# A self product computed as a fifth seven-block relation, and matrix sums moved to accumulating transfers

## The reference, cut to what matters

```python
# layer 0: three hops over a row-normalised adjacency
cur = h = x @ W + b;  out = dw[0] * h
for i in range(3):
    cur = adj @ cur;  out = out + dw[i+1] * cur
x = x + relu(out);  h = relu(layernorm(x))
# layer 1: four relations, 16384 weighted edges
for r in range(4):
    total_msg += (h[src] @ W_rel[r] + b_rel[r]) * where(edge_type == r, edge_weight, 0)[:, None]
agg = segment_sum(total_msg, dst) / maximum(segment_sum(edge_weight, dst), 1)[:, None]
h1 = h @ W_self + b_self + agg            # then layernorm, a feed-forward block, layernorm
```

## Time and profile before

| what | value |
|---|---|
| time before, median of 3 runs | 346.32 us (345.88 to 346.45) |
| the profiled execution's own time | 345.88 us |
| its span | 343.6 us |
| TensorE busy | 336.5 us (98% of the span) |
| VectorE busy | 243.2 us (71%) |
| GpSimd busy | 153.0 us (45%) |
| ScalarE busy | 87.1 us (25%) |
| chain that ended last, by engine | TensorE 88%, VectorE 8%, ScalarE 1% |
| granted TensorE clock | 0.9 or more of full speed in every slice |

### The profile page before, as it was taken

The page is one execution under the profiler, slowest core; times in us unless marked ns, Lnnn a source line. Parts: engine busy times, 40 slices in busy tenths (PEclk is TensorE's granted clock), DMA queues, the critical chain, the costliest instruction groups (busy, mean ns, idle before and its releaser), DMA issues.

```text
span 343.6 us, 4413 instructions
## 1 busy us (share of the span) xinstructions
PE 336.5 (98%) x1624; PEld 239.5 (70%) x1625; DVE 243.2 (71%) x428; ACT 87.1 (25%) x187; POOL 153.0 (45%) x122
## 2 busy tenths in 40 slices
PE   7999999999999999999999999999999999999996
PEld 3459887785478888888888888844774544474455
DVE  5899999988596898691484598786676555443543
ACT  3565664333410000000001062223352331112110
POOL 6000000461379999999936220491115440772020
PEclk9999999999999999999999999999999999999999
DMA  7100002728800000062300089942000000000003
GB/s 240 66 1 2 5 2 85 284 57 216 279 0 2 0 1 0 2 245 65 59 0 2 0 283 190 139 141 73 1 2 0 1 0 0 2 0 0 2 0 124
DMA packets 18630, 22.07 MB, mean 64 GB/s; under 512 B 2032, under 2 KB 10992, under 8 KB 18608
## 3 DMA queue, kind: packets, MB, share of 16 engines
q1 hardware_dynamic: 17936, 20.72, 21.6%
q0 software_dynamic: 240, 0.79, 0.8%
q10 hardware_dynamic: 432, 0.26, 0.2%
HBM read 20.72 MB, written 1.05 MB: 63 GB/s over the span
## 4 chain that ended last, share of the span: by engine, by line
PE 88%; DVE 8%; ACT 1%; DMA 1%; issue 1%; ACTq 0%; DVEq 0%
PE bank L1887 14%; PE bank L1736 14%; PE bank L1679 14%; PE bank L1616 8%; PE bank L1776 7%; PE bank L1843 6%; PE bank L1927 4%; PE bank L603 4%; PE bank L576 4%; PE bank L1875 4%; PE bank L600 3%; PE bank L1603 2%; PE bank L592 2%; DMA bias<-in_edge_type 1%; DVE stats L1209 1%; DVE h L1241 1%
## 5 line engine op out<-in xcount | busy, mean ns | idle before, releaser
L1051 ACT ACTIVATE columns<-mean_var,eps 128x1 f32<-128x1 f32 x16 | 4.7, 292 | 109.4 <-DVE mean_var L1210 109.3
L1736 PE MATMUL bank<-slots,wall 128*128 128x256 f32 x128 | 30.2, 380 | 0.0
L603 PE MATMUL bank<-slots 128*128 128x112 bf16 x256 | 27.8, 228 | 0.0
L907 POOL TENSOR_TENSOR slots<-slots 128x512 f32<-128x512 f32 x1 | 1.3, 1293 | 58.7 <-DMA slots<-in_L_gnn_W_rel 58.7
L1736 PEld LDWEIGHTS bank<-slots,wall 128*128 128x128 f32 x128 | 24.2, 190 | 3.2
L600 PE MATMUL bank<-slots 128*128 128x140 bf16 x128 | 26.2, 242 | 0.0
L386 DVE TENSOR_TENSOR slots<-slots 128x1792 bf16<-128x1792 bf16 (+1 forms) x27 | 25.0, 979 | 0.0
L1679 PE MATMUL bank<-slots,h_t 128*128 128x256 f32 x104 | 24.5, 380 | 0.0
L603 PEld LDWEIGHTS bank<-slots 128*128 128x128 bf16 x256 | 22.5, 103 | 2.7
L1887 PE MATMUL bank<-wall,h_t 128*128 128x512 f32 x48 | 22.4, 596 | 0.4 <-ACT slots L1160 0.4
L1679 PEld LDWEIGHTS bank<-slots,h_t 128*128 128x128 f32 x104 | 19.7, 190 | 3.1 <-issue 0.5
(11 more groups left out here) (293 smaller groups left out, 799.6 us busy)
## 6 DMA issues: line engine op xcount, KB each, us to landing
slots<-in_L_gnn_W_rel SPq DMA_DIRECT2D x4, 1024.0 KB, 9.6
spare<-in_L_gnn_W_ffn SPq DMA_DIRECT2D x1, 2048.0 KB, 8.0
slots<-in_L_gnn_W_ffn SPq DMA_DIRECT2D x1, 2048.0 KB, 9.1
slots<-in_L_gnn_Wr SPq DMA_DIRECT2D x8, 256.0 KB, 9.1
x<-in_x SPq DMA_DIRECT2D x4, 256.0 KB, 5.7
bias<-in_L_gnn_W SPq DMA_DIRECT2D x2, 512.0 KB, 5.0
slots<-in_L_gnn_W_self SPq DMA_DIRECT2D x1, 1024.0 KB, 5.3
bias<-in_L_gnn_b_rel SPq DMA_DIRECT2D x4, 256.0 KB, 8.4
```

What stands on the lines that cost most here:

```text
L603: ins = pe.matmul(place[:, :, 0:R, 0:WIDE].rearrange("p h r d -> p r h d"), low, wgt_hot[:, s, v, a, :, :, j], start=False, stop=False, sk ...
L1736: ins = pe.matmul(into, left[:, k, tile(p)], right[:, k, :], start=(n in (0, 2, 3, 5) and r == 0 and k == 0), stop=False, skip_group_check ...
```

## The change

1. The self product becomes a fifth seven-block relation. The list is now `rel_weight = [wself] + wrel`, `rel_out = [own_out] + msg`, numbered `q = 0..4`; the self relation is `q = 0` and its result goes to a new tensor `own_out`.
2. The five relations no longer run strictly one after the other. P1 and P2 of the first three are made ahead, in halves, between the transposes of `h`, into three different banks; the rest of the first three is interleaved. Relations 3 and 4 run in the old order.
3. VectorE no longer runs `keep_self`; the self bias goes in with the relation's steps. `own_out` is added to `h` by one accumulating transfer that GpSimd issues. GpSimd's four bias additions are gone.
4. The running sums over the weight matrices and the count halves are transfers that GpSimd issues: one 1 MB copy and three accumulating transfers of 1 MB, then two folds of 0.5 and 0.25 MB; for the counts 0.5 MB copied, 0.5 MB and 0.25 MB accumulated. Each waits for the one before it on its own sum.
5. Three of the four `split_projection` instructions (tiles 1 to 3) move from VectorE to GpSimd (`proj_split`); `finish_build` now runs ahead of `combine_rel(0)`, behind a wait for VectorE's `acc_ready`.
6. In the third hop TensorE takes tile pair (0, 3) ahead of (1, 1), and VectorE runs `scale_and_shift(0)` ahead of the last `add_hop` of the second hop.
7. `sum_weights(r, ...)` moves one relation later with its numbering: it lies in relations q = 2, 3, 4 and behind them.
8. SyncE's row loads are reordered: the five relation biases first.

```diff
@@ tensors and names @@
+own_out = between.enter_context(nc.sbuf_tensor("own_out", [P, NT, D], F32))
-        in_slot = slots[:, 7, :].rearrange("p (a k n) -> p a k n", k=2, n=HALF)
+        in_slot = slots[:, 0, :].rearrange("p (a k n) -> p a k n", k=2, n=HALF)
+        rel_weight, rel_bias, rel_out = [wself] + wrel, [bself] + brel, [own_out[:]] + msg
+        rel_bank = [[psum[i] for i in row] for row in ((0, 3, 6, 7), (1, 3, 6, 7), (2, 3, 6, 7), (0, 1, 2, 3), (0, 1, 2, 3))]
+        REL_SEQ = [(q, n) for n in (P1, P2) for q in range(AHEAD)]
+        REL_SEQ += [(0, P5), (0, P6), (0, P7), (1, P6), (0, P4), (0, P3), (1, P7), (1, P5), (1, P4), (1, P3)]
+        REL_SEQ += [(2, n) for n in (P6, P7, P5, P4, P3)]
+        REL_SEQ += [(q, n) for q in range(AHEAD, RELS) for n in (P1, P6, P7, P5, P2, P4, P3)]
@@ SyncE @@
             sp.wait_ge(built, 2)
-            for to, of in ((bself, bself_in), (g1, g1_in), (be1, be1_in), (g2, g2_in), (be2, be2_in), (bf2, bf2_in)):
-                sp.dma_start(to, row(of)).then_inc(rows_loaded, 16)
+            sp.dma_start(bself, row(bself_in)).then_inc(rel_rows_loaded, 16)
             for r in range(R):
                 sp.dma_start(brel[r], row(brel_in[r])).then_inc(rel_rows_loaded, 16)
+            for to, of in ((g1, g1_in), (be1, be1_in), (g2, g2_in), (be2, be2_in), (bf2, bf2_in)):
+                sp.dma_start(to, row(of)).then_inc(rows_loaded, 16)
@@ GpSimd @@
-            combine_rel(0)
-            finish_build()
-            pool.wait_ge(rows_loaded, 16 * 6)
-            for t in range(NT):
-                pool.wait_ge(t_ready, use_of(H_REL, t) + 1)
-                pool.tensor_tensor(h[:, t, :], h[:, t, :], bself, ALU.add).then_inc(self_biased, 1)
-            pool.wait_ge(hop_ready, HOPS * NT)
-            pool.wait_ge(node_s_ready, 3)
-            combine_rel(1)
-                for t in range(NT):
-                    with_this = wall[:, 0, t, :] if r == 1 else wgt_sum[:, t, :]
-                    pool.tensor_tensor(wgt_sum[:, t, :], with_this, wall[:, r, t, :], ALU.add).then_inc(wgt_add, 1)
...
+            pool.wait_ge(late_kept, LATE_COUNTS)
+            for m in range(1, NT):
+                pool.wait_ge(proj_out, m + 1)
+                pool.tensor_tensor(lo[0][:, m, :], h[:, m, :], hi[0][:, m, :].bitcast(F32), ALU.subtract).then_inc(proj_split, 1)
+            pool.wait_ge(acc_ready, NT)
+            finish_build()
+            combine_rel(0)
+            def add_weights(r):
+                pool.wait_ge(wgt_add, 16 * r)
+                pool.dma_start(wgt_sum[:], wall[:, r], accum_op=ALU.add).then_inc(wgt_add, 16)
+            pool.wait_ge(hop_ready, 2 * NT)
+            pool.dma_start(wgt_sum[:], wall[:, 0]).then_inc(wgt_add, 16)
+            pool.dma_start(cnt_sum[:], wall[:, R, 0:2, :]).then_inc(cnt_add, 16)
+            add_weights(1)
+            pool.wait_ge(cnt_add, 16)
+            pool.dma_start(cnt_sum[:], wall[:, R, 2:4, :], accum_op=ALU.add).then_inc(cnt_add, 16)
+            add_weights(2)
+            pool.wait_ge(cnt_add, 32)
+            pool.dma_start(cnt_sum[:, 0, :], cnt_sum[:, 1, :], accum_op=ALU.add).then_inc(cnt_add, 16)
             pool.wait_ge(hop_ready, HOPS * NT)
+            pool.wait_ge(node_s_ready, SUMS)
+            add_weights(3)
             combine_rel(1)
             combine_rel(2)
+            pool.wait_ge(wgt_add, 16 * R)
+            pool.dma_start(wgt_sum[:, 0:2, :], wgt_sum[:, 2:4, :], accum_op=ALU.add).then_inc(wgt_add, 16)
+            pool.wait_ge(msg_out, rel_step(0, STEPS))
+            pool.dma_start(h[:], own_out[:], accum_op=ALU.add).then_inc(own_added, 16)
+            combine_rel(3)
             combine_messages(0)
+            combine_rel(4)
             combine_messages(1)
@@ VectorE @@
                 moments(TO_REL, m, x[:, m, :])
+                scale_and_shift(TO_REL, m)
                 if m == 0:
                     add_hop(HOPS - 1, NT - 1)
-                scale_and_shift(TO_REL, m)
+                if m == 2:
+                    keep_right(0)
+                    keep_right(1)
+            keep_right(2)
...
+            for q in range(RELS):
+                if q > 0:
+                    dve.wait_ge(msg_out, rel_step(q - 1, STEPS))
+                link(dve.tensor_tensor(bias_step, rel_bias[q][:, side[0]], rel_bias[q][:, side[1]], ALU.subtract))
+                if q >= AHEAD:
+                    keep_right(q)
+                if q >= 2:
+                    sum_weights(q - 2, 0)
...
@@ TensorE @@
-                    order = [(0, 0), (0, 1), (0, 2), (1, 0), (1, 1), (0, 3), (1, 2), (1, 3)]
+                    order = [(0, 0), (0, 1), (0, 2), (1, 0), (0, 3), (1, 1), (1, 2), (1, 3)]
+                    if i == 1 and s > 0:
+                        pe.wait_ge(proj_split, s)
...
+            transposed(H_REL, 0)
+            first_half(0, 0)
+            first_half(1, 0)
+            fill_h(H_REL, 1, h_ready[TO_REL])
+            pe.wait_ge(wrel_loaded[2], 16)
+            first_half(2, 0)
+            transposed(H_REL, 1)
+            first_half(0, 1)
+            first_half(1, 1)
+            fill_h(H_REL, 2, h_ready[TO_REL])
+            first_half(2, 1)
+            second(0)
+            second(1)
+            fill_h(H_REL, 3, h_ready[TO_REL])
+            second(2)
+            for q, n in REL_SEQ[2 * AHEAD:]:
...
+                elif n == P6:
+                    pe.wait_ge(node_s_ready, 2)
+                    pe.wait_ge(rel_t_ready, 4 * q + 2)
+                    if q > 0:
+                        pe.wait_ge(msg_out, rel_freed(q, 1))
+                    block_product(p6, s2, t2, True)
...
+                elif n == P4:
+                    pe.wait_ge(msg_out, rel_step(q, 3))
+                    pe.wait_ge(rel_t_ready, 4 * q + 4)
+                    block_product(p74, a22, t4, False)
+                else:
+                    pe.wait_ge(msg_out, rel_step(q, 4))
+                    pe.wait_ge(node_s_ready, 4)
+                    block_product(p53, s4, b22, False)
```

More of the change, by code:

```diff
@@ L59 @@
 GROUPS = 4
+RELS = R + 1
+AHEAD = 3
 ADDS = 8
@@ L98, in gnn_program @@
             cnt_b = between.enter_context(nc.sbuf_tensor("cnt_b", [P, NT, N], BF16))
+        with ExitStack() as between:
+            own_out = between.enter_context(nc.sbuf_tensor("own_out", [P, NT, D], F32))
         cnt_r = sb("cnt_r", [P, NT, N], F32R)
@@ L114, in gnn_program @@
                        proj_out, hi_ready, lo_ready, sym_ready, x_in, src_in, dst_in, typ_in, wgt_in, w0_in, b0_in)
-        run_blocks(nc, sem, block, wall, tails, late_kept, block_out, x, ident, ones, eye, eps, load_flag, psum, slots, h, h_t, spare, adj, cnt_r, both_ways, bias,
+        run_blocks(nc, sem, block, wall, tails, late_kept, block_out, x, ident, ones, eye, eps, load_flag, psum, slots, h, h_t, spare, adj, cnt_r, own_out, both_ways, bias,
                    inv_cnt, hi, lo, b0, dw, dw_sum, b0_loaded, dw_loaded, acc_ready, steps_summed, built, proj_out, hi_ready, lo_ready, sym_ready,
@@ L518, in _ @@
                     dve.tensor_copy(wall[:, R, t, :], psum[NT + t]).then_inc(slow_cnt_out, 1)
-                for m in range(2):
-                    split_projection(m)
+                split_projection(0)
                 dve.wait_ge(proj_out, NT)
@@ L692, in ffn_place, with run_blocks @@
     return FFN_TILES.index(t)
-def run_blocks(nc, sem, block, wall, tails, late_kept, block_out, x, ident, ones, eye, eps, load_flag, psum, slots, h, h_t, spare, adj, cnt_r, both_ways, bias,
+def run_blocks(nc, sem, block, wall, tails, late_kept, block_out, x, ident, ones, eye, eps, load_flag, psum, slots, h, h_t, spare, adj, cnt_r, own_out, both_ways, bias,
                inv_cnt, hi, lo, b0, dw, dw_sum, b0_loaded, dw_loaded, acc_ready, steps_summed, built, proj_out, hi_ready, lo_ready, sym_ready, dw_in, wself_in, bself_in, wrel_in, brel_in,
@@ L1272, in _, with rel_parts, rel_sides, keep_right @@
                     add_hop(i, NT - 1)
+            def rel_parts(q):
+                return [bank[:].rearrange("p (k n) -> p k n", k=2) for bank in rel_bank[q]]
+            def rel_sides(q):
+                return [rel_bias[q][:, side[j]].unsqueeze(1).broadcast_to([P, 2, HALF]) for j in range(2)]
+            def keep_right(q):
+                dve.wait_ge(rel_rows_loaded, 16 * RELS)
+                dve.wait_ge(msg_ready, rel_made(q, P1))
+                dve.tensor_tensor(quarter(rel_out[q], 0, 1), rel_parts(q)[0], rel_sides(q)[1], ALU.add).then_inc(msg_out, 1)
             for m in range(NT):
@@ L1665, in _ @@
                         hop(m, s)
-            pe.wait_ge(wself_loaded, 16)
-            for m in range(NT):
-                transposed(H_REL, m)
-                pairs = rows_by(wself, m)
-                product(main[m][:], pairs[:KT - 1], stop=False)
-                if m + 1 < NT:
-                    fill_h(H_REL, m + 1, h_ready[TO_REL])
-                product(main[m][:], pairs[KT - 1:], start=False).then_inc(self_ready, 1)
```

(39 more changed lines are left out.)

202 lines of the change are left out of this document (85 added, 117 removed).

## The result

The changed kernel takes 354.83 us (median of 4 runs, 354.19 to 355.25), the kernel before 346.14 (345.88 to 346.45) beside it: ratio 1.025, 95% interval 1.023 to 1.027. It is slower by 8.7 us. The forecast was 344.9, the range 344.0 to 349.8: wrong in sign, and outside the range.

A forecast was written before the change was run, and what follows sets the result against it. TensorE, busy 98% of the span, and its wait for the first normalised tile were taken as the bound; -2.0 - 0.65 - 0.1 + 0.75 + 0.5 + 0.1 = -1.4 us gave a median of 344.9 us, range 344.0 to 349.8.

The forecast's parts named there:

- Transfers instead of GpSimd's additions, +0.1 us: Weight and count sums as transfers: removing GpSimd's additions gains nothing; P6 of relation 1 waits 0 to 0.1 us.
- the point of decision: On GpSimd ahead of `combine_rel(1)`: transfers in by 95.7 us cost 0 to 0.1, later ones cost one for one.
- a rival with 30%: Accumulating transfers move bytes twice, 8.0 us per MB; TensorE waits 4.9 us before P6 of relation 1: 349.8; chance 30%.
- 1.8 us of room: SyncE's loads beside GpSimd's transfers were taken to cost the 1.8 us left between 93.9 and 95.7, so no wait.
- The self product, -2.0: On TensorE, seven block products of 12.1 us replace the plain self product of 14.1 us: -2.0 us.
- The first tile, -0.65: Third hop: an earlier tile pair (0.46) and an earlier reciprocal (0.19) bring the first normalised tile 0.65 us earlier.
- The first hop, -0.1: VectorE loses three splits to GpSimd and its adjacency instructions start earlier: -0.1 us, bounds -0.3 and +1.0.
- The short price: GpSimd's splits in the first hop at 1.27 us each, not 1.72 beside VectorE; the third ready at 60.5 us.
- Relations between the transpositions, +0.75: TensorE waits 0.6 us for the second tile, 0.15 more for the third and fourth: +0.75 us, bounds 0.6 and 1.2.
- VectorE's lag, +0.5: Interleaved relations: VectorE's steps late by 0.15 in relation 1, 0.3 in relation 2, 0.05 for P3; bounds 0 and 3.3.

The follow-up runs named there:

- second to fourth experiments: Each from the changed kernel: copies in place of GpSimd's accumulating transfers, 346.08 us; SyncE's later loads waiting for the third weight transfer, 345.16; both edits, 347.26 (single run).

## Why the prediction was wrong

**The step that failed is "Transfers instead of GpSimd's additions, +0.1 us".** Its structure was right: which transfer GpSimd stands for, which product waits, the point of decision (95.7; the last node sum ended at 95.83), the first issue (74.1; it came at 74.00), and even the row that would decide it. It did not name the count fold, which also waits ahead of `combine_rel(1)`. The price was wrong twice, and something was missing: in place of +0.1 the runs show 8.1 us of wait and 2.5 of slower clock.

- *The price of an addition.* The text took a plain load's 5.3 us per MB and called the other price, twice the bytes, a rival with 30%. The second to fourth experiments show 205 GB/s for additions against 380 to 420 for copies. The rival was the right mechanism. No row of before could decide it; the rule from the Trainium skill (Collectives: The Full Stack, in the section cited beside the rival) came out, and had got too little weight.
- *The loads beside it.* The text gave them 1.8 us of room and said they would be gone by 90. They were gone by then (from 90 to 94 the rate is 221 GB/s, nearly that of additions alone), but by the table they had cost 7.6 to 9.0 us; with copies the third landing was at 97.4, not at 93.9. Both streams want the same 16 engines, already busy 0.80 of this stretch: the sum should have been one of the engines' time, which gives these sizes, and not one of latencies. The rival put the landing at 100.6, near the 103.8 measured, but partly by luck: with most of the loads away it came at 94.8, so the rival's chain of latencies was 5.8 too long, and it had nothing for the 9.0 of the loads. The wait is 8.1 us, not its 4.9, and its range (346.5 to 351) fell short.
- *The clock.* A gap of 8 us was priced as 8 us. It is 10.6: the granted clock behind it is 0.50, and the kernel with TensorE kept busy gives the 2.5 us back.

**The steps ahead of P6 held**, together -1.7 us in the changed kernel and -1.9 with the issues behind the block sums (P6 of relation 1 at 99.09), where -2.0 was said:

- The self product, -2.0: there are 56 instructions more under the relations' line and none of 512 columns; no run undid this step alone.
- The first tile, -0.65: its two moves alone gave 0.5 in the time and 0.61 in the row. In the changed kernel the transposition is at 79.98, 0.69 earlier than the earlier trace rows with the first hop's gain.
- The first hop, -0.1: GpSimd's splits ended at 60.7 and VectorE stood 1.03 us for them, but its own row inverses come at 60.91 instead of 61.01, 0.1 earlier. The short price was the right choice.
- Relations between the transpositions, +0.75: the gap ahead of the second tile is 0.36 (0.6 said). P5 of relation 0 starts at 94.10 (93.9 said), and the node sums took 0.69 each, not 1.23, as said.

**VectorE's lag, +0.5, was too small.** In the changed kernel it is 0.8, all at P4 of relation 2, but there VectorE could catch up in the wait of 8 us. With that wait gone it is 2.1 in the profiled execution: 0.60 in relation 1 (0.15 said), 0.79 in relation 2 (0.3 said), and 0.75 in relation 3, which the text had catching up. The total lies within its bounds (0 and 3.3). With the block sums earlier about 0.9 is left.

Without the transfers' step the sum was -1.5. The kernel that takes their wait out (issues behind the block sums) measures -1.0, and -1.2 with the block sums earlier. About 0.4 of that lies outside the span: the median span goes from 343.7 to 343.0 and 342.8, so inside it the gain is 0.7 and 0.9. In the profiled execution with the issues behind the block sums -1.9 and +2.1 meet, and its span is 343.7, as before; how long the lag is in its faster executions isn't recorded.

## What to carry to other kernels

A transfer that the issuing engine has to wait for is an instruction of that engine, as long as the transfer: put it behind everything on that engine that others wait for. Price several transfers that run together as the time they keep the DMA engines busy, with an accumulating one at about twice its bytes, and not as a chain of single landings read in a quiet stretch. And when a wait can open in front of TensorE, price the slower clock behind it too.

## What the runs showed of the hardware beyond this

- The granted clock fell to its lower level (1.2 of 2.4 GHz) behind gaps of 8.0 and 2.1 us and cost 2.5 and about 1.8 us. Behind 1.67 it stayed high in the profiled execution. In five of that kernel's twelve runs the clock of the whole span is 0.995, as where it fell behind 2.1; behind which gap it fell in them isn't recorded. Behind 1.15 and 0.53 the rows show it high.
- GpSimd's issue of an accumulating transfer took 0.85 to 0.90 us alone and up to 1.54 right behind others, that of a copy 0.53 to 0.71.
- VectorE's steps with both inputs in on-chip memory took 2.4 to 2.8 us in four places (116.60 and 121.02 above, and one each in the two fastest kernels) where GpSimd issued a transfer and started a sum right behind it. Beside an issue with nothing behind it such a step was not slowed (0.69 us at 95.14, beside the issue at 95.02), and steps that read a TensorE bank were not slowed by either. What holds the step, the issue or the sum queued behind it, stays open.
- The execution's time exceeds its span by 2.3 us in the kernel before and in its variant with the first tile's moves, and by 1.8 us in the changed kernel (354.98 against 353.2). By medians it is 2.2 to 2.3 against 1.9 to 2.0 in the versions of the changed kernel. So 0.4 us of what the fast versions gain lies outside the span, and no run here explains it.
